# Buffers of a hybrid attention, expert and state-space kernel begin at multiples of 64 bytes

## The chip, the core and the metric

The kernel runs on one core of a Trainium2 chip. The metric is the device time of one execution in microseconds (us). A core has five engines that work side by side: TensorE (PE, matrix products; its weight loads are shown apart as PEld), VectorE (DVE), ScalarE (ACT), GpSimd (POOL) and SyncE (SP), which starts the DMA transfers. They meet through semaphores alone.

## The reference, cut to what matters

Four layers work on x, 1024 tokens of 256 features, each on a layer-normalised x and each added back to it:

```python
x = x + attention(layernorm(x), wq, wk, wv, wo)     # 16 heads of 128, 4 key heads, 4 sink keys + window of 32
x = x + experts(layernorm(x), ...)                  # 8 LoRA experts on one 704-wide gated FFN, top 2
x = x + mixer(layernorm(x), ...)                    # 512 inner, 4 heads, state 64, convolution of 4, output product
x = x + experts(layernorm(x), ...)                  # the same weights again

# attention
q = (x @ wq.T); k = (x @ wk.T); v = (x @ wv.T)
scores = q @ k.T / sqrt(128)                        # masked: k <= q and (k < 4 or k >= q - 31)
out = softmax(scores) @ v @ wo.T

# experts, for each expert e
h_e = silu(base_up + lo_up) * (base_gate + lo_gate)
mixed_h += c[:, None] * h_e;  lora_down += 2 * (c[:, None] * h_e @ down_A[e].T @ down_B[e].T)
out = mixed_h @ w_down.T + lora_down
```

All of it is in float32.

## The kernel before, in words

**Two-part products.** Most products run in TensorE's reduced float32 format (F32R). An operand is kept as a high part, rounded to that format, and a low part, the remainder. The helper `three` (line 168) issues three matmuls for a product: high with high, high with low, low with high. Line 172 is its `e.matmul`, so nearly all heavy matmuls stand under L172. Buffers of such pairs have names that end in `_hl`. ScalarE writes high parts, VectorE (in some places GpSimd) low parts. Scores, transposes and the mixer's inner products are plain float32 matmuls.

**A matmul's operands.** One operand is loaded into the array (PEld), 128 columns or so; the other is streamed, 66 to 512 columns. In the profile's names `psum<-A,B` A is streamed and B is loaded. The load for the next matmul runs beside the streaming of the present one.

**Layout.** On-chip memory is laid out by hand. Small constants, the residual x and statistics are placed by `keep` from byte 16512 of each partition on, in steps of 32. Behind them begin the large areas A_X to A_WO (lines 139 to 151), each followed by the next, and all four stages place their buffers in these areas by `at(name, shape, type, offset)`:

- A_X: `xT_hl`, the normalised and transposed x. Every stage streams it (attention also loads its first block).
- A_V: `v_hl` in attention; from the first experts' stage on `ffn_w_hl`, all weights of that stage, 61,440 bytes. The mixer's `ssd_w_out_hi` lies right behind.
- A_K: `kT`. A_KW: `k_windows`, the key blocks. A_PR: `probs`.
- A_W: `wq_hl`, and in other stages `f_ch_hl`, `f_mix_hl`, `f_sil` and mixer buffers. A_Q: `qT`, `f_um`, mixer weights and working buffers.
- A_O: `oT_hl`, before it `xg_hl`, `wk_hl`. A_P: `probs_first`, `probs_wide`. A_PT: `pT_hl`. A_WO: `wo_hl`, `wv_hl`.

**Attention** goes through 44 units, 4 key heads by 11 query blocks (the first of 128 queries, the others of 90). For a window unit GpSimd gathers a key block: 4 sink keys and three windows of 62 into `k_windows` (L773, L775); TensorE computes three score products of 66 columns (L493); VectorE masks (L697) and takes the row maximum, ScalarE exponentiates (L602), GpSimd multiplies by the reciprocal and writes three 66-wide pieces into the zeroed 126-wide rows of `probs_wide` (L788, L789); TensorE transposes them (L525), ScalarE and VectorE split the result into `pT_hl`, and TensorE multiplies with `v_hl`. Values come from `xg_hl`, a copy of x with the sink columns before each window, 10 rows of 126 columns for each part and half. Between these, the order written by hand puts the query products of the next head (xT_hl with wq_hl) and the output products (wo_hl with oT_hl).

**An experts' stage** takes 12 steps, 6 blocks of the hidden width for each of two halves of the tokens. A step issues 12 matmuls of xT_hl with ffn_w_hl (`base_x`), 12 of f_um with ffn_w_hl (`base_lora`, `second`), 6 of f_ch_hl with ffn_w_hl and 12 of ffn_w_hl with f_mix_hl (`down`). ScalarE and VectorE work on the step before meanwhile. **The mixer** has 20 input products (xT_hl with its weights), then 8 chunks of 128 tokens.

Nothing plans the order at run time: each engine runs its own written list and waits on semaphores.

## Time and profile before

| | |
|---|---|
| Median of 3 runs | 521.92 us (521.79 to 522.21) |
| The profiled execution's own time | 522.12 us |
| Its span, first to last instruction | 520.3 us |
| TensorE matmuls busy | 503.9 us, 97% of the span |
| TensorE weight loads busy | 426.7 us, 82% |
| VectorE busy | 408.8 us, 79% |
| ScalarE, GpSimd busy | 312.8 us, 145.4 us |
| Granted TensorE clock | 1.0 of full speed in all slices |

Busy time is the union of an engine's instructions; matmuls overlap, since one begins while the one before is still on its way through the array. A matmul's own duration is therefore longer than its distance to the next one; the distance (start to start) is what a sequence costs. In a view in order of time, instructions that follow each other with the same names are merged into one row with their count, and the difference of two rows' starts gives the time of the whole group between.

The reduced-precision matmuls, by the pair of names (streamed, loaded), with the count in the view of groups and the places of the two buffers modulo 64 bytes, worked out from the layout constants (offsets inside the buffers are multiples of 64, but for xg_hl, whose rows of 504 bytes begin at various places):

| Pair | Columns | Count | Places now | Places after the change |
|---|---|---|---|---|
| xT_hl, ffn_w_hl | 512 | 312 | 32, 32 | 0, 0 |
| f_um, ffn_w_hl | 512 | 288 | 0, 32 | 0, 0 |
| xT_hl, wq_hl | 512 | 192 | 32, 0 | 0, 0 |
| f_ch_hl, ffn_w_hl | 512 | 136 | 0, 32 | 0, 0 |
| xT_hl, mixer input weights (116), router (16), wk_hl (48) | 512 | 180 | 32, 0 | 0, 0 |
| wv_hl, xg_hl (60) and xT_hl (6) | 512 | 66 | 0, various or 32 | 0, 0 |
| pT_hl, v_hl | 512 | 12 | 0, 32 | 0, 0 |
| wo_hl, oT_hl | 256 | 384 | 0, 0 | 0, 0 |
| ffn_w_hl, f_mix_hl (272) and f_d_hl (48) | 256 | 320 | 32, 0 | 0, 0 |
| ssd_w_out_hi, g_hi and g_lo | 256 | 64 | 32, 0 | 0, 0 |
| pT_hl, v_hl | 360 | 120 | 0, 32 | 0, 0 |

The pairs with unequal places are 874 matmuls of 512 columns, 384 of 256 and 120 of 360.

### The profile page before, as it was taken

To read this page: it belongs to the slowest core of one execution; us is meant where nothing else is said; L and a number is where in the kernel's file an instruction comes from. 1 tells how busy PE (TensorE), PEld (TensorE's weight loads), DVE (VectorE), ACT (ScalarE), POOL (GpSimd) and SP (SyncE) were. 2 spreads that over 40 slices of the span, in tenths; PEclk is the share of its full clock that TensorE was granted. 3 is DMA by queue.
4 is the path that set the end of the run, shared out by engine and by line. 5 is a ranking of instruction groups with operands and counts; after the bars stand their busy time and mean duration, and the time that the engine had idled before them with its cause. 6 is when DMAs were issued, how large, how long until landed. Compare 5 with 4: busy or idle time off the path is not lost.

```text
span 520.3 us, 9035 instructions
## 1 busy us (share of the span) xinstructions
PE 503.9 (97%) x2950; PEld 426.7 (82%) x2951; DVE 408.8 (79%) x899; ACT 312.8 (60%) x784; POOL 145.4 (28%) x285
## 2 busy tenths in 40 slices
PE   6999999999999999999999999989999999999996
PEld 5778899999999988678888888867989768888885
DVE  5736567667666799899999899986788789899777
ACT  4656878688687754664534445899872365334342
POOL 1332424245243320020110111389554020020110
PEclk9999999999999999999999999999999999999999
DMA  7320100000000303000030000000000000000101
GB/s 273 128 82 1 42 2 2 1 1 2 2 2 15 144 2 117 31 1 1 0 141 2 2 0 1 1 2 1 1 2 1 0 0 3 1 0 1 40 2 40
DMA packets 5933, 14.17 MB, mean 27 GB/s; under 512 B 640, under 2 KB 3200, under 8 KB 5888
## 3 DMA queue, kind: packets, MB, share of 16 engines
q1 hardware_dynamic: 5888, 13.60, 7.4%
q8 instruction: 24, 0.39, 0.3%
q14 instruction: 21, 0.17, 0.1%
HBM read 12.55 MB, written 1.05 MB: 26 GB/s over the span
## 4 chain that ended last, share of the span: by engine, by line
PE 74%; DVE 15%; issue 4%; ACT 4%; DMA 1%; POOL 1%; SPq 0%; DVEq 0%; ACTq 0%; POOLq 0%
PE psum L172 57%; PE psum L493 4%; DVE xs L1993 2%; PE psum L525 2%; DVE f_t L1315 1%; PE psum L1808 1%; DMA w_raw<-in_wk 1%; PE psum L1812 1%; DVE ln_stats L214 1%; PE psum L1818 1%; PE psum L241 1%; DVE f_ch L1384 1%; DVE f_ch_hl L1398 1%; DVE xn L234 1%; DVE xT_hl L257 1%
## 5 line engine op out<-in xcount | busy, mean ns | idle before, releaser
L172 PE MATMUL psum<-xT_hl,ffn_w_hl 128*128 128x512 f32 x312 | 77.7, 395 | 0.7 <-ACT f_sil L1201 0.6
L172 PE MATMUL psum<-f_um,ffn_w_hl 128*128 128x512 f32 x288 | 72.9, 399 | 1.1 <-DVE f_t L1315 0.6
L172 PEld LDWEIGHTS psum<-xT_hl,ffn_w_hl 128*128 128x128 f32 x312 | 56.2, 188 | 13.1 <-DVE ffn_w_hl L916 1.1
L172 PEld LDWEIGHTS psum<-f_um,ffn_w_hl 128*128 128x128 f32 x288 | 53.1, 188 | 15.0 <-DVE f_um L1327 1.8
L1201 ACT ACTIVATE f_sil<-psum 128x512 f32<-128x512 f32 (+1 forms) x48 | 28.2, 596 | 48.9 <-PE psum L172 48.9
L1225 ACT ACTIVATE f_ch_hl<-f_ch 128x512 fp32r<-128x512 f32 x48 | 30.3, 632 | 42.3 <-DVE f_ch L1384 40.6
L172 PE MATMUL psum<-xT_hl,wq_hl 128*128 128x512 f32 x192 | 52.1, 407 | 0.6 <-ACT qT L593 0.6
L172 PE MATMUL psum<-wo_hl,oT_hl 128*128 128x256 f32 x384 | 50.6, 281 | 0.9 <-DVE oT_hl L726 0.6
L172 PEld LDWEIGHTS psum<-wo_hl,oT_hl 128*128 128x128 f32 x384 | 47.9, 188 | 3.4 <-DVE oT_hl L726 1.1
L593 ACT ACTIVATE qT<-psum 128x512 f32<-128x512 f32 x32 | 35.2, 1101 | 22.6 <-PE psum L172 22.6
L602 ACT ACTIVATE probs<-probs,small 120x66 f32<-120x66 f32 x120 | 39.8, 338 | 8.2 <-DVE small L703 8.2
L1315 DVE TENSOR_TENSOR f_t<-psum,f_sil 128x512 f32<-128x512 f32 (+1 forms) x48 | 33.1, 690 | 14.4 <-ACT f_sil L1201 13.3
L172 PEld LDWEIGHTS psum<-xT_hl,wq_hl 128*128 128x128 f32 x192 | 33.9, 188 | 7.7 <-issue 1.7
L788 POOL TENSOR_TENSOR probs_wide<-probs,small 120x186 f32<-120x186 f32 x40 | 19.9, 498 | 68.6 <-DVE small L683 68.6
L697 DVE TENSOR_TENSOR probs<-psum,const_bf_bits 120x198 f32<-120x198 f32 x40 | 14.5, 361 | 27.4 <-PE psum L493 27.4
L1398 DVE TENSOR_TENSOR f_ch_hl<-f_ch,f_ch_hl 128x512 fp32r<-128x512 f32 (+1 forms) x48 | 35.6, 779 | 0.1
L1384 DVE TENSOR_TENSOR f_ch<-f_t,f_wb 128x512 f32<-128x512 f32 x48 | 33.2, 691 | 1.4
L172 PEld LDWEIGHTS psum<-ffn_w_hl,f_mix_hl 128*128 128x128 f32 x240 | 30.8, 188 | 2.2 <-DVE f_mix_hl L1407 0.5
L172 PE MATMUL psum<-f_ch_hl,ffn_w_hl 128*128 128x512 f32 x120 | 32.1, 400 | 0.6 <-DVE f_ch_hl L1398 0.5
L1496 POOL MEMSET f_t<- 64x512 f32 x8 | 4.2, 519 | 101.7 <-DVE f_ch L1384 101.7
L172 PE MATMUL psum<-ffn_w_hl,f_mix_hl 128*128 128x256 f32 x240 | 31.6, 280 | 0.0
L172 PE MATMUL psum<-pT_hl,v_hl 126*128 126x360 f32 (+1 forms) x132 | 30.5, 339 | 0.0
(265 smaller groups left out, 1149.1 us busy)
## 6 DMA issues: line engine op xcount, KB each, us to landing
w_raw<-in_wq SPq DMA_DIRECT2D x4, 512.0 KB, 4.1
w_raw<-in_wo SPq DMA_DIRECT2D x4, 512.0 KB, 3.2
ffn_w_raw<-in_ffn SPq DMA_DIRECT2D x3, 576.0 KB, 5.4
ffn_w_raw_far<-in_ffn SPq DMA_DIRECT2D x3, 576.0 KB, 5.0
ssd_w_raw<-in_ssd SPq DMA_DIRECT2D x3, 512.0 KB, 5.4
x_resid<-in_x SPq DMA_DIRECT2D x2, 512.0 KB, 5.3
out_x<-x_resid SPq DMA_DIRECT2D x4, 256.0 KB, 2.1
w_raw<-in_wk SPq DMA_DIRECT2D x1, 512.0 KB, 6.3
```

What stands on the lines that cost most here:

```text
L172: i = e.matmul(dst, lhs(a), rhs(b), start=start and n == 0, stop=stop and n == len(TERMS) - 1, **kw)
L493: m = e.matmul(bank(u % 2)[0:ROWS, i * KBLK:(i + 1) * KBLK], queries_of(q, QB), kw[:, w % W_SLOTS, i, :], start=True, stop=True)
L525: m = e.transpose(bank(2 + u % 2)[0:NKEY, i * ROWS:(i + 1) * ROWS], pz[0:ROWS, u % 3, i, :], ident[0:ROWS, 0:ROWS])
L593: e.activation(qT[:, HALF * half:HALF * half + HALF, h], bank(7 if n == Q_PAIR else 6), ACT.Copy, scale=float(HD) ** -0.5).then_inc(s_qt, 1)
L602: m = e.activation(p[:, n, :], p[:, n, :], ACT.Exp, bias=NEGM[0:rows, u % 4, n:n + 1], accum_out=DEN[0:rows, u % 4, n:n + 1])
L697: e.tensor_tensor(masked, bank(u % 2)[0:rows, 0:n].rearrange("p (n k) -> p n k", n=parts), (cb[0:rows, B_M0:B_M1] if j == 0 else cb[0:rows ...
L788: e.tensor_tensor(wide, p[:, :, SINK:KBLK], spread(r, KB_WIN), ALU.mult)
L1201: e.activation(sil[at_rows, s, :], bank(i % 2)[rows, :], ACT.Silu).then_inc(FS[f"sil{s}"], 1)
L1225: e.activation(ch_hl[:, i % 2, s, HI, :], ch[:, i % 2, s, :], ACT.Copy).then_inc(FS["chh"], 1)
L1315: e.tensor_tensor(tt[rows, s, :], to_bank(i, 1)[rows, :], sil[rows, s, :], ALU.mult).then_inc(FS[f"t{s}"], 1)
L1384: e.tensor_tensor(ch[:, i % 2, s, :], tt[:, s, :], wb[:, s, half(h)], ALU.mult).then_inc(FS[f"ch{s}"], 1)
L1398: e.tensor_tensor(ch_hl[rows, i % 2, s, LO, :], ch[rows, i % 2, s, :], f32(ch_hl[rows, i % 2, s, HI, :]), ALU.subtract).then_inc(FS["chl"], 1)
```

## The change

Every large area begins at a multiple of 64 bytes; the padding before A_W shrinks by 544 bytes, so that A_W, A_Q, A_O and A_P stay at their addresses. The rows of `xg_hl` and `probs_wide` get a pitch of 128 elements (512 bytes) for their 126, those of `k_windows` a pitch of 80 elements (320 bytes) for their 66. The instructions read and write the same elements as before; only the clearing of `probs_wide` covers the padding too.

| Area | Begins at, before | after |
|---|---|---|
| A_X, A_V, A_K, A_KW | 30752, 47136, 92192, 108576 (32 modulo 64) | 32 higher (0 modulo 64) |
| A_PR | 110976 | 111488 |
| A_W, A_Q, A_O, A_P | 114432, 147200, 163584, 196352 | the same |
| A_PT, A_WO | 202944, 211136 (0 modulo 64) | 64 higher |

```diff
@@ -136,20 +136,26 @@
         minus_half = keep("minus_half", [P, NT], F32)
         small = keep("small", [P, 256], F32)
         sm = keep("softmax_small", [P, 48], F32)
-        R = base[0]
-        A_X = R
+        LINE = 64
+
+        def lines(n):
+            return -(-n // LINE) * LINE
+
+        A_X = lines(base[0])
         A_V = A_X + 2 * KB * T * 4
         A_K = A_V + 2 * NJ * KV * HD * 4
         A_KW = A_K + KV * T * 4
-        A_PR = A_KW + -(-(W_SLOTS * NB_Q * KBLK * 4) // 32) * 32
-        A_W = A_PR + -(-(3 * NB_Q * KBLK * 4) // 32) * 32 + 1056
+        KEY_PITCH, WINDOW_PITCH = lines(NKEY * 4) // 4, lines(KBLK * 4) // 4
+        A_PR = A_KW + W_SLOTS * NB_Q * WINDOW_PITCH * 4
+        A_W = A_PR + lines(3 * NB_Q * KBLK * 4) + 512
         A_Q = A_W + 32768
         A_O = A_Q + 16384
         A_P = A_O + 32768
-        A_PT = A_P + 2048 + -(-(3 * NB_Q * NKEY * 4) // 32) * 32
+        A_PT = A_P + 2048 + 3 * NB_Q * KEY_PITCH * 4
         A_WO = A_PT + 8192
         END = A_WO + 16384
         assert END <= 229344, END
+        assert all(a % LINE == 0 for a in (A_X, A_V, A_K, A_KW, A_PR, A_W, A_Q, A_O, A_P, A_PT, A_WO))
 
         ident = cf[:, C_ID:C_ID + P]
         identb = cb[:, B_ID:B_ID + P]
@@ -284,19 +290,19 @@
 
         def attention():
             kT = at("kT", [P, KV, T], F32, A_K)
-            kw = at("k_windows", [P, W_SLOTS, NB_Q, KBLK], F32, A_KW)
+            kw = at("k_windows", [P, W_SLOTS, NB_Q, WINDOW_PITCH], F32, A_KW)
             v_hl = at("v_hl", [P, 2, NJ, KV * HD], F32R, A_V)
             wq_hl = at("wq_hl", [P, 2, 2, KB, HALF], F32R, A_W)
             raw = at("w_raw", [P, 4, 1024], F32, A_W + 16384)
             qT = at("qT", [P, T, GROUP], F32, A_Q)
             oT_hl = at("oT_hl", [P, 2, GROUP, T], F32R, A_O)
-            xg_hl = at("xg_hl", [P, 2, KB, NJ - 1, NKEY], F32R, A_O)
+            xg_hl = at("xg_hl", [P, 2, KB, NJ - 1, KEY_PITCH], F32R, A_O)
             wk_hl = at("wk_hl", [P, 2, KB, KV * HD], F32R, A_O + 20480)
             wv_hl = at("wv_hl", [P, 2, KB, KV * HD], F32R, A_WO + 8192)
             wo_hl = at("wo_hl", [P, 2, 2, GROUP, D], F32R, A_WO)
             pr = at("probs", [P, 3, NB_Q, KBLK], F32, A_PR)
             pr0 = at("probs_first", [P, NB_Q0, P], F32, A_P)
-            pz = at("probs_wide", [P, 3, NB_Q, NKEY], F32, A_P + 2048)
+            pz = at("probs_wide", [P, 3, NB_Q, KEY_PITCH], F32, A_P + 2048)
             pT_hl = at("pT_hl", [P, 2, 2, 512], F32R, A_PT)
             NEGM, DEN, DENG, RDEN = (small[:, 192 + 16 * i:208 + 16 * i].rearrange("p (b h) -> p b h", b=4) for i in range(4))
 
@@ -491,7 +497,7 @@
                         for i in range(NB_Q):
                             q = Q0[j] + QB * i
                             m = e.matmul(bank(u % 2)[0:ROWS, i * KBLK:(i + 1) * KBLK], queries_of(q, QB),
-                                         kw[:, w % W_SLOTS, i, :], start=True, stop=True)
+                                         kw[:, w % W_SLOTS, i, 0:KBLK], start=True, stop=True)
                     m.then_inc(s_s, 1)
 
                 for j in range(NJ):
@@ -506,7 +512,7 @@
                         e.wait_ge(s_vlo, j - 1)
                     for k in range(KB):
                         m = three(e, bank(4 + j % 2)[0:NK[j], :],
-                                  lambda w: xT[:, w, k, 0:P] if j == 0 else xg_hl[:, w, k, j - 1, :],
+                                  lambda w: xT[:, w, k, 0:P] if j == 0 else xg_hl[:, w, k, j - 1, 0:NKEY],
                                   lambda w: wv_hl[:, w, k, :], k == 0, k == KB - 1)
                     m.then_inc(s_v, 1)
                     if j < GROUP:
@@ -523,7 +529,7 @@
                     else:
                         for i in range(NB_Q):
                             m = e.transpose(bank(2 + u % 2)[0:NKEY, i * ROWS:(i + 1) * ROWS],
-                                            pz[0:ROWS, u % 3, i, :], ident[0:ROWS, 0:ROWS])
+                                            pz[0:ROWS, u % 3, i, 0:NKEY], ident[0:ROWS, 0:ROWS])
                     m.then_inc(s_t, 1)
 
                 def p_v(u):
@@ -784,7 +790,7 @@
                     if u >= 3:
                         e.wait_ge(s_t, u - 2)
                     z = pz[0:rows, u % 3]
-                    wide = bass.AP(z.tensor, z.offset + SINK, [z.ap[0], (NKEY + QB, NB_Q), (1, KB_WIN)])
+                    wide = bass.AP(z.tensor, z.offset + SINK, [z.ap[0], (KEY_PITCH + QB, NB_Q), (1, KB_WIN)])
                     e.tensor_tensor(wide, p[:, :, SINK:KBLK], spread(r, KB_WIN), ALU.mult)
                     e.tensor_tensor(z[:, :, 0:SINK], p[:, :, 0:SINK], spread(r, SINK), ALU.mult).then_inc(s_nrm, 1)
 
```

## Rows read from the trace of the kernel before

**Rows 1.** The page: busy time, share and instructions; then slices in tenths.

```profile
PE 503.9 (97%) x2950; PEld 426.7 (82%) x2951; DVE 408.8 (79%) x899; ACT 312.8 (60%) x784; POOL 145.4 (28%) x285
...
PE   6999999999999999999999999989999999999996
...
DVE  5736567667666799899999899986788789899777
```

**Rows 2.** The page: the chain that ended last, shares by engine.

```profile
PE 74%; DVE 15%; issue 4%; ACT 4%; DMA 1%; POOL 1%; SPq 0%; DVEq 0%; ACTq 0%; POOLq 0%
```

**Rows 3.** Stretches: length, busy us (count) of PE, PEld, DVE, ACT, POOL; clock, DMA.

```profile
224.00:306.00 82.00, 81.79 (x416) 68.10 (x417) 77.43 (x135) 40.13 (x71) 9.09 (x13) 1.00 0.07 23
306.00:350.00 44.00, 42.29 (x216) 33.86 (x217) 41.49 (x78) 32.10 (x58) 15.89 (x38) 1.00 0.00 1
```

**Rows 4.** TensorE in order of time: start us, us, what; one feed-forward step.

```profile
257.32 2.89 PE L172 MATMUL psum<-xT_hl,ffn_w_hl 128*128 128x512 f32 x12
260.05 2.96 PE L172 MATMUL psum<-f_um,ffn_w_hl 128*128 128x512 f32 x12
262.86 1.56 PE L172 MATMUL psum<-f_ch_hl,ffn_w_hl 128*128 128x512 f32 x6
264.26 1.56 PE L172 MATMUL psum<-ffn_w_hl,f_mix_hl 128*128 128x256 f32 x12
265.66 0.63 PE L172 MATMUL psum<-xT_hl,ffn_w_hl 128*128 128x512 f32 x2
```

**Rows 5.** TensorE in order of time, attention.

```profile
106.86 1.53 PE L172 MATMUL psum<-wo_hl,oT_hl 128*128 128x256 f32 x12
108.22 0.66 PE L172 MATMUL psum<-pT_hl,v_hl 126*128 126x360 f32 x3
108.72 0.47 PE L525 MATMUL psum<-const_f,probs_wide 120*126 120x120 f32 x3
```

**Rows 6.** TensorE in order of time, the mixer's input products.

```profile
321.69 2.96 PE L172 MATMUL psum<-xT_hl,ssd_w_z_hl 128*128 128x512 f32 x12
324.49 0.86 PE L172 MATMUL psum<-xT_hl,ssd_w_conv_hl 128*128 128x512 f32 x3
```

**Rows 7.** Groups of instructions: busy us, mean ns, idle before.

```profile
L172 PE MATMUL psum<-xT_hl,ffn_w_hl 128*128 128x512 f32 x312 | 77.7, 395 | 0.7 <-ACT f_sil L1201 0.6
L172 PE MATMUL psum<-f_um,ffn_w_hl 128*128 128x512 f32 x288 | 72.9, 399 | 1.1 <-DVE f_t L1315 0.6 <-DVE f_um L1327 0.5
...
L1384 DVE TENSOR_TENSOR f_ch<-f_t,f_wb 128x512 f32<-128x512 f32 x48 | 33.2, 691 | 1.4
...
L788 POOL TENSOR_TENSOR probs_wide<-probs,small 120x186 f32<-120x186 f32 x40 | 19.9, 498 | 68.6 <-DVE small L683 68.6
...
L655 DVE COPY kT<-psum 128x512 f32<-128x512 f32 x8 | 5.1, 683 | 0.6 <-PE psum L172 0.6
```

**Rows 8.** TensorE in order of time, plain float32: attention, then the mixer.

```profile
36.69 1.13 PE L486 MATMUL psum<-kT,qT 128*128 128x128 f32 x8
37.58 0.70 PE L172 MATMUL psum<-wv_hl,xg_hl 128*126 128x512 f32 x2
...
364.88 1.05 PE L1808 MATMUL psum<-w_mix,x_dt 128*128 128x128 f32 x8
365.76 1.06 PE L1812 MATMUL psum<-c_exp,state 128*128 128x128 f32 x8
```

**Rows 9.** TensorE in order of time, two runs behind scores.

```profile
131.11 1.66 PE L172 MATMUL psum<-wo_hl,oT_hl 128*128 128x256 f32 x12
132.61 0.63 PE L172 MATMUL psum<-pT_hl,v_hl 128*128 128x512 f32 x2
...
134.18 1.62 PE L172 MATMUL psum<-wo_hl,oT_hl 128*128 128x256 f32 x12
135.64 0.66 PE L172 MATMUL psum<-pT_hl,v_hl 126*128 126x360 f32 x3
```

## The prediction

> **What bounds the kernel now.** I read the busy shares first, then the chain of waits, the stretches, and last single runs of matmuls on TensorE's timeline. TensorE's matmul side is busy 503.9 of 520.3 us, 97%, and nearly every slice stands at 9, while VectorE is at 79% [rows 1]. The chain of work that ended last is 74% TensorE and 15% VectorE [rows 2]. In the steady part of the first feed-forward stage TensorE is busy 81.79 of 82 us and VectorE 77.43; in the mixer's input part it is 42.29 of 44, with VectorE at 41.49 [rows 3]. So time is gained or lost here by the distance from one matmul to the next, and hardly by anything else.
>
> This distance depends on more than the columns. All four runs of one feed-forward step follow each other without a wait [rows 4]. Twelve matmuls of 512 columns, xT_hl against ffn_w_hl, take 260.05 - 257.32 = 2.73 us, 227.5 ns each. The next twelve, of the same shape, f_um against ffn_w_hl, take 2.81 us, 234.2 ns each; six of f_ch_hl take 1.40 us, 233.3 ns. Twelve of 256 columns, ffn_w_hl against f_mix_hl, take 1.40 us, 116.7 ns, where in attention twelve of wo_hl against oT_hl take 1.36 us, 113.3 ns [rows 5]. In the mixer twelve of xT_hl against ssd_w_z_hl take 2.80 us, 233.3 ns [rows 6]. (A name pair gives the streamed operand first and the loaded one second.)
>
> What sorts the fast from the slow is the two addresses modulo 64, worked out from the kernel's constants. xT_hl, ffn_w_hl, v_hl, kT and ssd_w_out_hi begin 32 bytes past a multiple of 64; wq, wk, wv, wo, oT_hl, f_um, f_ch_hl, f_mix_hl, pT_hl and the mixer's input weights begin at a multiple. Fast are xT_hl with ffn_w_hl (both at 32) and wo_hl with oT_hl (both at 0). Slow are 0 with 32 (f_um, f_ch_hl) and 32 with 0 (f_mix_hl, the mixer). Neither operand's own place explains it: ffn_w_hl is loaded in a fast and in two slow kinds, xT_hl is streamed in a fast and a slow kind. Only equal or unequal places do.
>
> **The change part by part.** It moves A_X, A_V, A_K and A_KW up by 32 bytes, and A_PT and A_WO by 64. A_PR to A_P stay put or stay at 0 modulo 64. After it every pair of the table ahead is "equal". It adds no instruction, no wait and no semaphore, and moves no DMA past a queue; the raw weights land where they did.
>
> *1. Unequal pairs of reduced-precision matmuls become equal.* By the table there are 874 of 512 columns, 384 of 256 and 120 of 360. Upper bound: each goes from the unequal to the equal pace. 512 columns: 233.8 - 227.5 = 6.3 ns (233.8 is the middle of 234.2 and 233.3), 874 x 6.3 = 5.5 us. 256 columns: 116.7 - 113.3 = 3.4 ns, 384 x 3.4 = 1.3 us. 360 columns: three take 108.72 - 108.22 = 0.50 us, 166.7 ns [rows 5], against 227.5 x 360 / 512 = 160.0, 120 x 6.7 = 0.8 us. Together 7.6 us. Lower bound: over the whole trace the equal group costs 77.7 / 312 = 249.0 ns a matmul and the unequal one 72.9 / 288 = 253.1, both with their tails [rows 7]; the difference is 4.1 ns, since equal runs too need a few matmuls to reach their pace. 874 x 4.1 = 3.6 us, half of it for 256 columns 384 x 2.0 = 0.8, seven tenths for 360 columns 120 x 2.9 = 0.3: 4.7 us. I take 5.0, 2.7 and 5.0 ns, nearer to the first steady rows but not at them, because with all neighbours equal fewer runs should have to start over: 4.4 + 1.0 + 0.6 = 6.0 us.
>
> *2. What of this reaches the end.* In the steady feed-forward stretch VectorE leaves 82 - 77.43 = 4.6 us, and the stretch holds 82 / 8.34 = 9.8 steps [rows 4] with 18 unequal matmuls of 512 columns and 12 of 256 each: 177 x 5.0 + 118 x 2.7 = 1.2 us, which passes whole. In the mixer's input part VectorE leaves 44 - 41.49 = 2.5 us, unevenly, and TensorE already waits 1.7 us; of its 116 input matmuls and the last step's 18 and 12, and f_d_hl's 24, 134 x 5.0 + 36 x 2.7 = 0.8 us, I count half. In the kernel's first 25 us (wk's 48 matmuls and wv's 6) and around the two routers (some 48), TensorE keeps waiting for inputs, means and masks: 102 x 5.0 = 0.5 us is not passed on. Off: 0.9 us. 6.0 - 0.9 = 5.1 us.
>
> *3. The gathered inputs' rows of 504 bytes become 512.* These are the 60 matmuls with xg_hl as the loaded operand and are in the 874. ScalarE writes the same number of elements into them.
>
> *4. Key blocks at 320 in place of 264 bytes, widened probabilities at 512 in place of 504.* These feed plain fp32 matmuls (240 scores, 120 transposes), for which the place shows nothing: eight unequal ones, kT against qT, take 37.58 - 36.69 = 0.89 us, 111.3 ns, and eight equal ones, w_mix against x_dt, take 365.76 - 364.88 = 0.88 us, 110.0 ns [rows 8]. I take nothing; the bound from both sides is 1.3 ns on 392 such matmuls (with the 32 of kT), 0.5 us.
>
> *5. The other engines' reads and writes at the new places.* VectorE writes 512 columns to kT at 32 in 683 ns and to f_ch at 0 in 691 [rows 7]: nothing, bounded at 8 ns on some 40 such instructions on the chain, 0.3 us either way. GpSimd's products into the widened probabilities keep their length, with 68.6 us idle before them [rows 7] to cover what differs. The one memset over them grows from 1134 to 1152 columns, under 2% of an instruction that runs while TensorE waits for its first input.
>
> The Trainium skill ("SBUF — State Buffer", section "A bandwidth-pool intuition that's wrong (but worth ruling out)") gives TensorE a second, independent read port for loading weights. By that rule the two operands' relative place would not matter and part 1 would be worth nothing. The rows on equal and unequal pairs disagree with it. Its remark in "Door 1: The DMA port swizzle (why `[64,N]` ≈ `[32,N]`)" on lines of 16 bytes speaks against the change as well, since places 0 and 32 both begin such a line; the unequal pace in the rows is not explained by it either.
>
> The profiled execution took 522.12 us, 1.8 us more than its span, and lies 0.2 us above the runs' median of 521.92. 522.12 - 5.1 = 517.0, as a median **516.8 us**.
>
> **The rivals.**
> *A. VectorE takes over.* Its share is 94% in two stretches [rows 3], and the chain already passes through it for 15% [rows 2]. A step's partial results come in the order PE, ScalarE, VectorE, PE, so a faster TensorE may only wait longer. Against it: TensorE waits 0.21 us in 82. If the feed-forward stages and the mixer give back what they gain, attention remains, 192 matmuls with wq, 60 with xg_hl and 12 + 120 of pT_hl: 264 x 5.0 + 120 x 5.0 = 1.9 us, and 0.4 us of the last stage's: 2.3 us, 519.6 us.
>
> *B. The address is not the cause.* The pace may come from the order of instructions or from what ran before. For it: one equal run, wo_hl with oT_hl at 131.11, takes 1.50 us, and one in the same position behind scores, at 134.18, 1.46 us [rows 9]: 3.6 ns apart on the eleven behind the first, with the same addresses modulo 64. So phase matters as well. Against it: all the long unequal runs shown are slow, in three stages. Time: no change, 521.9 us. This is also what the skill's rule of two independent ports would give.
>
> *C. Slower: equal runs fall into the slow phase.* The run at 131.11 shows that equal places do not guarantee the fast pace. With all buffers moved together, and the unequal runs between them gone that now reset the phase, the 312 + 384 matmuls that are fast today could stay at the slow pace: 312 x 6.7 + 384 x 3.6 = 3.5 us lost, with nothing won on the others. Half of them so gives 1.7 us, 523.6 us. It decides as soon as more matmuls leave the fast pace than enter it.
>
> *D. All of it.* Every unequal run reaches the steady equal pace and short runs start in it: 7.6 us, less 0.2 behind VectorE: 514.5 us.
>
> **How the numbers follow.** Forecast (515.2 to 518.7) 0.57; A (518.7 to 520.9) 0.16; B 0.10; C 0.09; D 0.08. A difference under 0.2% (1.04 us, about what measurements of this kernel can tell from none) counts as none. Faster: forecast, A and D, 0.81, less 0.01 of A: 0.80. None: B and the 0.01: 0.11. Slower: C, 0.09. The range takes in D and A and leaves out most of B and C: 514.2 to 520.8 us; the bounds of parts 4 and 5 (0.8 us) are within it.
>
> **What would show it.** In a feed-forward step, f_um's twelve in 2.72 to 2.76 us, f_ch_hl's six in 1.37 and f_mix_hl's twelve in 1.36 to 1.37; the mixer's twelve in 2.73; xT_hl with ffn_w_hl unchanged. Scores and transposes as before. If the feed-forward paces fall and the stretch does not, A. If they stay at 234, B, and the prediction is wrong at its root. If xT_hl's twelve rise to 2.80, C. A faster pace in plain fp32 matmuls, or other durations on VectorE, would prove parts 4 and 5 wrong.

## The result, and the profile after

The changed kernel takes 523.52 us (median of 10, 523.26 to 523.75) against 522.13 us (521.79 to 522.21) for the kernel before beside it: ratio 1.0027, interval 1.0019 to 1.0035. It is 1.4 us slower; forecast were 5.1 us gained and a range that ended at 520.8 us. The span of the profiled execution went from 520.3 to 521.6 us.

The page of the changed kernel says that the bound is the same, with a busier TensorE: 504.8 us against 503.9, VectorE 408.7 against 408.8 [rows 1], and 77% of the chain on TensorE against 74% [rows 2].

```profile
PE 504.8 (97%) x2950; PEld 428.0 (82%) x2951; DVE 408.7 (78%) x899; ACT 313.9 (60%) x784; POOL 145.6 (28%) x285
...
PE 77%; DVE 14%; issue 4%; ACT 3%; POOL 1%; DMA 1%; DVEq 0%; SPq 0%; ACTq 0%; POOLq 0%
```

Its groups (busy us, mean ns) name the loser. wo_hl with oT_hl stood at 50.6 us in the kernel before (first line below) and is at 52.1. wq, slow before, gained 0.3 us (52.1 before). The feed-forward pairs and the other engines are where they were [rows 7]. All line numbers of TensorE's helper are six higher now.

```profile
L172 PE MATMUL psum<-wo_hl,oT_hl 128*128 128x256 f32 x384 | 50.6, 281 | 0.9 <-DVE oT_hl L726 0.6
...
L178 PE MATMUL psum<-xT_hl,ffn_w_hl 128*128 128x512 f32 x312 | 78.0, 397 | 0.7 <-ACT f_sil L1207 0.6
L178 PE MATMUL psum<-f_um,ffn_w_hl 128*128 128x512 f32 x288 | 72.7, 398 | 1.1 <-DVE f_t L1321 0.6
...
L178 PE MATMUL psum<-wo_hl,oT_hl 128*128 128x256 f32 x384 | 52.1, 285 | 0.9 <-DVE oT_hl L732 0.6
L178 PE MATMUL psum<-xT_hl,wq_hl 128*128 128x512 f32 x192 | 51.8, 406 | 0.6 <-ACT qT L599 0.6
...
L794 POOL TENSOR_TENSOR probs_wide<-probs,small 120x186 f32<-120x186 f32 x40 | 20.0, 499 | 69.5 <-DVE small L689 69.5
...
L1390 DVE TENSOR_TENSOR f_ch<-f_t,f_wb 128x512 f32<-128x512 f32 x48 | 33.2, 691 | 1.4
```

TensorE in order of time (start us, us, what) shows a run's pace as the difference of two starts. In attention wo's twelve take 61.97 - 60.53 = 1.44 us, 120 ns each, where they took 1.36 [rows 5]; both runs behind scores take 1.50 and 1.51 us, where one had 1.46 [rows 9]. A feed-forward step is 266.83 - 258.45 = 8.38 us against 8.34 [rows 4]: f_um's twelve 2.80, f_ch's six 1.40, f_mix's twelve 1.41, all as slow as before, and xT_hl's twelve, said to stay, 2.77 against 2.73. In the mixer twelve take 2.75 us against 2.80 [rows 6], the only long run that gained. Eight plain records take 0.89 us against 0.88 [rows 8].

```profile
60.53 1.60 PE L178 MATMUL psum<-wo_hl,oT_hl 128*128 128x256 f32 x12
61.97 0.69 PE L178 MATMUL psum<-pT_hl,v_hl 126*128 126x360 f32 x3
...
131.44 1.67 PE L178 MATMUL psum<-wo_hl,oT_hl 128*128 128x256 f32 x12
132.94 0.86 PE L178 MATMUL psum<-pT_hl,v_hl 128*128 128x512 f32 x3
...
134.51 1.67 PE L178 MATMUL psum<-wo_hl,oT_hl 128*128 128x256 f32 x12
136.02 0.67 PE L178 MATMUL psum<-pT_hl,v_hl 126*128 126x360 f32 x3
...
258.45 2.93 PE L178 MATMUL psum<-xT_hl,ffn_w_hl 128*128 128x512 f32 x12
261.22 2.96 PE L178 MATMUL psum<-f_um,ffn_w_hl 128*128 128x512 f32 x12
264.02 1.56 PE L178 MATMUL psum<-f_ch_hl,ffn_w_hl 128*128 128x512 f32 x6
265.42 1.57 PE L178 MATMUL psum<-ffn_w_hl,f_mix_hl 128*128 128x256 f32 x12
266.83 2.93 PE L178 MATMUL psum<-xT_hl,ffn_w_hl 128*128 128x512 f32 x12
...
322.67 2.91 PE L178 MATMUL psum<-xT_hl,ssd_w_z_hl 128*128 128x512 f32 x12
325.42 0.85 PE L178 MATMUL psum<-xT_hl,ssd_w_conv_hl 128*128 128x512 f32 x3
...
365.89 1.05 PE L1814 MATMUL psum<-w_mix,x_dt 128*128 128x128 f32 x8
366.78 1.06 PE L1818 MATMUL psum<-c_exp,state 128*128 128x128 f32 x8
```

The table sorts the difference of 1.3 us by place in the program, and by pair from start-to-start distances (breaks in a run left out, the first matmuls of a run counted).

| part of the span | after - before, us | | pair | ns before, after | us |
|---|---|---|---|---|---|
| up to attention's first probabilities | -0.28 | | wo_hl, oT_hl | 115.1, 119.2 | +1.5 |
| attention | +1.20 | | xT_hl, ffn_w_hl | 229.3, 230.3 | +0.3 |
| first experts | +0.15 | | ffn_w_hl, f_mix_hl | 116.9, 117.8 | +0.2 |
| mixer | -0.02 | | xT_hl with wq, wk, mixer inputs | 233, 230 | -0.8 |
| second experts | +0.22 | | f_um and f_ch_hl, ffn_w_hl | 233.2, 233.4 | +0.1 |

Attention carries the loss and wo_hl with oT_hl carries attention's. A pair that the prediction counted among the gainers, wv_hl with xg_hl (60 matmuls), went from 231.8 to 233.0 ns.

### The profile page after: what moved, and what is told of

Its sections match the earlier page's. It is cut to its first block, busy times and chain, and to the rows that moved or that the text cites. A ratio compares the mean times of both kernels' runs of the same rounds, so it can differ in the third digit from the quotient of the medians.

```text
span 521.6 us, 9035 instructions
## 1 busy us (share of the span) xinstructions
PE 504.8 (97%) x2950; PEld 428.0 (82%) x2951; DVE 408.7 (78%) x899; ACT 313.9 (60%) x784; POOL 145.6 (28%) x285
## 4 chain that ended last, share of the span: by engine, by line
PE 77%; DVE 14%; issue 4%; ACT 3%; POOL 1%; DMA 1%; DVEq 0%; SPq 0%; ACTq 0%; POOLq 0%
PE psum L178 59%; PE psum L499 4%; PE psum L531 2%; DVE xs L1999 2%; PE psum L1814 1%; DVE f_t L1321 1%; PE psum L1818 1%; PE psum L1824 1%; DVE xT_hl L263 1%; PE psum L247 1%; DVE xn L240 1%; DVE f_ch_hl L1404 1%; PE psum L1841 1%; DVE ln_stats L220 1%; PE psum L492 1%
## 5 line engine op out<-in xcount | busy, mean ns | idle before, releaser
L178 PE MATMUL psum<-wo_hl,oT_hl 128*128 128x256 f32 x384 | 52.1, 285 | 0.9 <-DVE oT_hl L732 0.6
L178 PEld LDWEIGHTS psum<-wo_hl,oT_hl 128*128 128x128 f32 x384 | 49.3, 190 | 3.2 <-DVE oT_hl L732 1.1
```

What stands on the lines that cost most here:

```text
L178: i = e.matmul(dst, lhs(a), rhs(b), start=start and n == 0, stop=stop and n == len(TERMS) - 1, **kw)
```

## Experiments

In the expectations P is the theory that the distance between the two operands' places decides the pace. Its rival, S in the first texts and H in a later one, is that what runs ahead decides. D is VectorE as the next bound. "Distance" is from here on the loaded operand's address less the streamed one's, modulo 256. "Fast" and "slow" say of a run of wo's twelve whether its fourth to eleventh start-to-start times have a mean of 113 to 114 ns or of 117 to 118; the first three are left out, since many runs take them slower.

**wo_hl alone moved, in the kernel before.**

```diff
-        A_WO = A_PT + 8192
+        A_WO = A_PT + 8192 + 64
```

> The kernel before with A_WO alone 64 bytes higher; nothing else of the change. Theory P: the runs of wo_hl with oT_hl go from 1.36 to 1.43 us, all others keep their pace, +1.6 us, 523.7 us. Rival S (the loss comes from equal neighbours around these runs): the runs stay at 1.36 us, 522.1 us. Rival W (the widened rows cost the time): 522.1 us.

Measured 523.41 us, ratio 1.0027 (1.0016 to 1.0037): the whole loss of the change from one address. Only the pair wo_hl, oT_hl moved, from 115.1 to 119.4 ns (+1.5 us), all others stayed within 0.2 us. In this kernel's TensorE rows the run takes 62.09 - 60.66 = 1.43 us.

```profile
60.66 1.59 PE L172 MATMUL psum<-wo_hl,oT_hl 128*128 128x256 f32 x12
62.09 0.67 PE L172 MATMUL psum<-pT_hl,v_hl 126*128 126x360 f32 x3
```

Both operands are multiples of 64 in both kernels, so "equal modulo 64" says nothing here, and the prediction's rule is wrong.

**wo_hl put back, in the changed kernel.**

```diff
-        A_WO = A_PT + 8192
+        A_WO = A_PT + 8192 + 448
```

> The changed kernel with A_WO 448 bytes higher, so that wo_hl lies 192 bytes past a multiple of 512 again, as before the change (oT_hl lies 256 past one). Theory P (the place of the streamed operand relative to the loaded one counts over a period longer than 64 bytes, some hundred bytes, so that the move of wo_hl by 64 bytes against oT_hl lost the fast pace): a long run of wo_hl with oT_hl goes from 1.43 to 1.36 us for its twelve, the 384 matmuls give back 1.5 us, 522.0 us. Rival S (the slow phase is a matter of how runs follow each other, not of wo_hl's place): the runs stay at 1.43 us, 523.5 us.

Measured 522.69 us, ratio 1.0013 (1.0004 to 1.0022), between the two. Half of the loss came back. wo's mean is 116.9 ns: 17 of its 19 unbroken runs of twelve stand at 117 to 118 ns, where the kernel before has 18 at 113 to 114. The run in the rows takes 69.27 - 67.86 = 1.41 us. The distance is the same as before, so there is a second cause.

```profile
67.86 1.58 PE L178 MATMUL psum<-wo_hl,oT_hl 128*128 128x256 f32 x12
69.27 0.67 PE L178 MATMUL psum<-pT_hl,v_hl 126*128 126x360 f32 x3
```

**The pitches alone, in the kernel before** (the three new row lengths, each area kept at its old place modulo 512).

```diff
-            kw = at("k_windows", [P, W_SLOTS, NB_Q, KBLK], F32, A_KW)
+            kw = at("k_windows", [P, W_SLOTS, NB_Q, WINDOW_PITCH], F32, A_KW)
...
-            xg_hl = at("xg_hl", [P, 2, KB, NJ - 1, NKEY], F32R, A_O)
+            xg_hl = at("xg_hl", [P, 2, KB, NJ - 1, KEY_PITCH], F32R, A_O)
...
-            pz = at("probs_wide", [P, 3, NB_Q, NKEY], F32, A_P + 2048)
+            pz = at("probs_wide", [P, 3, NB_Q, KEY_PITCH], F32, A_P + 2048)
```

> The kernel before with the three wider row pitches alone (512 bytes for the gathered inputs and the widened probabilities, 320 for the key blocks); the areas keep their places modulo 512. Theory P: only the 60 matmuls with xg_hl may move, within 0.1 us: 522.1 us. Rival W (the pitches cost what the change lost, through scores, transposes or GpSimd): 523.5 us.

Measured 522.10 us against 521.98, ratio 1.0002 (0.9993 to 1.0011). No cost of the pitches can be told from none, and wo stays fast in 18 of 19 runs.

**A map of distances.** A micro kernel, traced once at a granted clock of 0.998: runs of 24 reduced-precision matmuls, each with its own weight load.

```diff
+                for k in range(n):
+                    m = e.matmul(PS[:, g % 6, 0:cols], pool[:, st:st + P], pool[:, mv:mv + cols], start=k == 0, stop=k == n - 1)
```

> Computes nothing of the reference; copies x to the output, and beside it issues groups of 24 reduced-precision matmuls, first of 512 and then of 256 streamed columns, every one with its own weight load of 128 columns. Between groups stands one matmul of 64 columns. The streamed operand lies at one place, the loaded one 64 KB and 0, 32, 64, ... 992 bytes further; then both are moved together by 32, 64, 128, 256 bytes. Theory P: the steady distance takes a few values, 226.7, 230 and 233.3 ns for 512 columns, 113.3, 116.7 and 120 ns for 256, and they depend on the relative place with a period above 64 bytes; moving both together changes nothing. Theory E of the prediction (equal or unequal modulo 64): two values that alternate from step to step. Rival N (no dependence on addresses): one value throughout.

The rows of this kernel: one matmul of 64 columns as a mark, then the 24. At distance 0 (first two rows) the 24 of 512 columns take 54.65 - 49.09 = 5.56 us, at 32 they take 5.68. With 256 columns distance 0 costs 278.62 - 275.67 = 2.95 us and distance 64 costs 2.82: the best place for 512 columns is among the worst two for 256.

```profile
49.09 5.71 PE L148 MATMUL psum<-operands 128*128 128x512 f32 x24
54.65 0.19 PE L146 MATMUL psum<-operands 128*128 128x64 f32 x1
54.67 5.84 PE L148 MATMUL psum<-operands 128*128 128x512 f32 x24
60.35 0.19 PE L146 MATMUL psum<-operands 128*128 128x64 f32 x1
...
275.67 3.12 PE L148 MATMUL psum<-operands 128*128 128x256 f32 x24
278.62 0.20 PE L146 MATMUL psum<-operands 128*128 128x64 f32 x1
...
281.61 2.98 PE L148 MATMUL psum<-operands 128*128 128x256 f32 x24
284.43 0.19 PE L146 MATMUL psum<-operands 128*128 128x64 f32 x1
```

Mean start-to-start time of the last 16, in ns, with the 360 columns of the next kernel:

| distance | 0 | 32 | 64 | 96 | 128 | 160 | 192 | 224 |
|---|---|---|---|---|---|---|---|---|
| 512 columns | 226.7 | 233.3 | 233.3 | 234.3 | 232.9 | 233.2 | 228.7 | 233.3 |
| 360 columns | 164.4 | 166.6 | 166.7 | 165.3 | 166.7 | 163.3 | 166.7 | 164.4 |
| 256 columns | 120.0 | 118.3 | 113.3 | 117.2 | 118.7 | 120.2 | 117.8 | 116.6 |

It repeats every 256 bytes up to 992 (tried for 512 and 256 columns). Moving both operands together, tried at distances 0 and 192, changes it by 0.8 ns at most. In steps finer than 32 bytes the next kernel has 226.7 ns at distance 240 for 512 columns, and 232.4 at 4. Most pairs of the two kernels stand near it:

| pair | distance before, after | ns by the map | ns measured |
|---|---|---|---|
| xT_hl, ffn_w_hl | 0, 0 | 226.7, 226.7 | 229.3, 230.3 |
| f_um and f_ch_hl, ffn_w_hl | 32, 64 | 233.3, 233.3 | 233.2, 233.4 |
| xT_hl with wq, wk, mixer inputs | 224, 192 | 233.3, 228.7 | 233, 230 |
| ffn_w_hl, f_mix_hl | 224, 192 | 116.6, 117.8 | 116.9, 117.8 |
| wo_hl, oT_hl | 64, 0 | 113.3, 120.0 | 115.1, 119.2 |

One pair does not: wv_hl with xg_hl stands at distance 0 after the change, where the map has 226.7 ns, and takes 233.0 in its runs of six.

**The feed-forward step, and plain matmuls, by distance.** Micro kernel, traced once, with the step of [rows 4]: u is the distance of f_um and f_ch_hl, f that of f_mix_hl.

```diff
+                for q, (mv, st, cols, n, plain) in enumerate(parts):
+                    as_ = (lambda a: a.bitcast(F32)) if plain else (lambda a: a)
```

> Computes nothing of the reference; copies x to the output and issues groups of matmuls: single kinds of 24 (360 columns, 512 columns at finer distances, 128 columns plain and reduced) at distances 0 to 224; then three feed-forward steps in a row (12 x 512 at distance 0, 12 x 512 and 6 x 512 at a distance u, 12 x 256 at a distance f) for u of 0, 32, 64, 192 and f of 0 to 224; then four attention steps in a row (6 x 512 at distance a, 12 x 256 at b, 3 x 360 at 0, 9 plain) for a of 0, 192, 224 and b of 0 to 224. Theory P: the feed-forward step is shortest for u = 0 and f = 64, 8.0 to 8.1 us, against 8.35 for u = 32, f = 224 (before) and 8.4 for u = 64, f = 192 (the change); plain matmuls show one pace. Rival S: the step's time does not follow the sum of the steady paces, and differs more between orders than between distances.

Three steps between two marks, in its rows, take 255.75 - 230.93 = 24.82 us at u 0, f 64; 581.62 - 556.53 = 25.09 at the old places (32, 224); 757.96 - 732.77 = 25.19 at the new ones (64, 192).

```profile
230.93 24.98 PE L149 MATMUL psum<-operands 128*128 128x512 f32 x126
255.75 0.20 PE L144 MATMUL psum<-operands 128*128 128x64 f32 x1
...
556.53 25.26 PE L149 MATMUL psum<-operands 128*128 128x512 f32 x126
581.62 0.19 PE L144 MATMUL psum<-operands 128*128 128x64 f32 x1
...
732.77 25.35 PE L149 MATMUL psum<-operands 128*128 128x512 f32 x126
757.96 0.19 PE L144 MATMUL psum<-operands 128*128 128x64 f32 x1
```

The middle step alone takes 8.33 us at the old places and 8.38 at the new, which is what the two whole kernels show (8.34, 8.38). The expected 8.0 to 8.1 us at u 0, f 64 was missed: the middle step takes 8.24 there and is shortest, 8.22, at u 0 with f 96 or 192. Theory P does not hold for the last run of the step. Behind six matmuls at u 0 the twelve of 256 columns at f 64 take 1.41 us, behind six at u 64 they take 1.37, where the map's 113.3 ns would make 1.36. The gain of the 512 columns is there: f_um's twelve take 2.72 us at u 0 and 2.80 at 32 or 64.

Records of 128 columns follow each other in 111.6 to 111.7 ns at every distance, plain or reduced. Four steps in attention's order take 21.06 to 21.37 us; wo's distance 64 is 0.15 to 0.21 us shorter than 0, and 192 is as short as 64 or shorter behind two of the three places of the run ahead.

**Places chosen by the map, in the changed kernel.** xT_hl, v_hl, wq_hl, ffn_w_hl, f_um, f_ch_hl, oT_hl and the mixer's input weights all at 0 modulo 256, wo_hl and ssd_w_out at 192, f_mix_hl at 64 (core of the edit; the tiles behind f_mix_hl move with it).

```diff
-        A_X = lines(base[0])
+        A_X = -(-base[0] // 256) * 256
...
-        A_WO = A_PT + 8192
+        A_WO = A_PT + 8192 + 192
...
-            mix_hl = at(f"{tag}_mix_hl", [P, 2, 2, HALF], F32R, A_W + 16384)
+            mix_hl = at(f"{tag}_mix_hl", [P, 2, 2, HALF], F32R, A_W + 16448)
```

> The changed kernel with places chosen by the map of the run before (distance of the loaded operand from the streamed one modulo 256): A_X, A_V, A_W, A_Q, A_O, A_PT at multiples of 256, so that all pairs of 512 columns lie at distance 0; f_mix_hl and its neighbours and the mixer's buffers behind them 64 bytes higher, wo_hl 64 bytes below a multiple, wv_hl at one, ssd_w_out_hi and _lo 64 below one, so that the pairs of 256 columns lie at distance 64. Theory P (the distance modulo 256 sets the pace): f_um's twelve in 2.73 us, f_mix_hl's in 1.36, the mixer's in 2.73; 7 us less by the steady paces, 5 us after what runs need to settle: 517 us, bounds 514.5 and 520. Rival S (how runs follow each other decides, and short runs never settle): the paces stay between, 521 us or more.

Measured 521.06 us against 522.10, ratio 0.9980 (0.9971 to 0.9989): faster than both kernels, but far from the 517 us of theory P and outside its bounds of 514.5 to 520; rival S had said 521 or more. f_um went from 233.3 to 228.1 ns (-1.4 us), f_ch_hl to 228.2 (-0.6), wq to 230.7 (-0.35), the mixer's inputs and wk to 228.5 (-0.6 together). A step in the second experts' stage takes 464.74 - 456.50 = 8.24 us, f_um's twelve 2.72, f_ch's six 1.36: the figures that the prediction expected of the change.

The pairs of 256 columns gained nothing. f_mix's twelve in this step take 1.41 us, not 1.36. Of the pair's 20 runs of twelve five reach 113 ns, the one at 455.13 among them (1.37 us); over the kernel the pair stands at 117.0 ns, where it had 116.9 before and the map has 113.3 for its distance of 64. The step in the micro kernel has the same times at the same places (1.41 of 8.24 us). wo stands at 115.9 ns against 115.1: 13 of its 19 runs take five matmuls at 116 to 123 ns before they reach 113, and three never do. f_d_hl, left at distance 0, went from 117.1 to 119.2. TensorE's busy time fell from 503.94 to 501.66 us, and the span by 1.2.

```profile
455.13 1.53 PE L178 MATMUL psum<-ffn_w_hl,f_mix_hl 128*128 128x256 f32 x12
456.50 2.91 PE L178 MATMUL psum<-xT_hl,ffn_w_hl 128*128 128x512 f32 x12
459.25 2.88 PE L178 MATMUL psum<-f_um,ffn_w_hl 128*128 128x512 f32 x12
461.97 1.52 PE L178 MATMUL psum<-f_ch_hl,ffn_w_hl 128*128 128x512 f32 x6
463.33 1.58 PE L178 MATMUL psum<-ffn_w_hl,f_mix_hl 128*128 128x256 f32 x12
464.74 2.91 PE L178 MATMUL psum<-xT_hl,ffn_w_hl 128*128 128x512 f32 x12
```

The second stage became 0.70 us shorter, the first, with the same matmuls, 0.12. The stretch of the first stage (length, busy us and count by engine; the kernel before, then this one) shows where it went: TensorE was busy 85.36 of 85.57 us and is busy 84.74 of 85.45. Of 0.62 us that it saves, 0.50 is idle time now, beside a VectorE at 80.70 in both.

```profile
231.66:317.23 85.57, 85.36 (x446) 71.02 (x445) 80.70 (x141) 39.67 (x69) 8.49 (x11) 1.00 0.06 22
...
231.22:316.67 85.45, 84.74 (x447) 71.11 (x445) 80.70 (x141) 39.66 (x70) 8.51 (x11) 1.00 0.06 22
```

**Is that VectorE?** The last kernel with four of the first stage's low parts made on GpSimd.

```diff
-                    if 1 <= i <= 4:
-                        split(i + 3)
...
+                if first:
+                    e.wait_ge(s_fwl, 4)
+                    for n in range(4, NPIECE):
+                        w_lo(e, n)
```

> The kernel with chosen places, and the low parts of the last four weight pieces (4.5 us of VectorE in the first experts' stage) made by GpSimd. Theory D (the first experts' stage hardly gained from the chosen places because VectorE holds it back there): that stage falls from 85.45 to 84.7 us and the kernel by 0.7 us, 520.3 us. Rival (the stage is held by something else, or GpSimd's reads slow VectorE): no change, 521.1 us, or slower.

Measured 523.19 us, ratio 1.0023 (1.0014 to 1.0033): 2.1 us slower than without the edit. The rows of GpSimd, VectorE and TensorE at that place (idle time and what ended it in brackets) show a product on VectorE (f_t times f_wb), 0.69 us elsewhere, lasting 2.68 us: it starts 0.56 us after GpSimd's operation of 2.69 us and ends 0.55 us behind it. TensorE waits 1.70 us for what follows from it.

```profile
226.74 2.69 POOL L922 TENSOR_TENSOR ffn_w_hl<-ffn_w_raw_far,ffn_w_hl 128x1152 fp32r<-128x1152 f32 x1 [2.09 <-ACT ffn_w_hl L918]
...
227.30 2.68 DVE L1390 TENSOR_TENSOR f_ch<-f_t,f_wb 128x512 f32<-128x512 f32 x1
...
232.12 1.63 PE L178 MATMUL psum<-f_ch_hl,ffn_w_hl 128*128 128x512 f32 x6 [1.70 <-DVE f_ch_hl L1404]
```

The edit gave VectorE less to do and held it up elsewhere, so it doesn't settle how much VectorE alone takes of the first stage's gain; that stays open.

**What holds wo's runs at 118 ns: the distance of wq_hl?** In the kernel before, wq_hl at distance 192 (the changed kernel's), then at 0.

```diff
-            wq_hl = at("wq_hl", [P, 2, 2, KB, HALF], F32R, A_W)
+            wq_hl = at("wq_hl", [P, 2, 2, KB, HALF], F32R, A_W - 32)
```

> The kernel before with wq_hl alone 32 bytes lower, so that the loaded operand of the query products lies 192 past the streamed one modulo 256, as after the change, and wo_hl stays at its old distance of 64 from oT_hl. Theory H (the place decides, but a run of twelve can also stay in the state in which the run before it leaves it): the query products fall from 233 to 230 ns, and the runs of wo_hl with oT_hl behind them rise from 113.3 to 117.7 ns although their own addresses did not change; +0.4 us in attention, 522.4 us. Rival P (distance alone): the runs of wo_hl stay at 113.3 ns and the kernel gains 0.3 us, 521.7 us.

Measured 522.17 us against 521.94 (0.9996 to 1.0014). The time can't be told from none, the runs can: wq gained 0.2 us by its own distance, and wo, none of whose addresses moved, lost 0.36, since 11 of its 19 runs of twelve now stand at 117 to 118 ns. Its run at 72.17 takes 1.42 us; the same run of the kernel before (first two rows) takes 1.38.

```profile
72.31 1.55 PE L172 MATMUL psum<-wo_hl,oT_hl 128*128 128x256 f32 x12
73.69 0.66 PE L172 MATMUL psum<-pT_hl,v_hl 126*128 126x360 f32 x3
...
72.17 1.58 PE L172 MATMUL psum<-wo_hl,oT_hl 128*128 128x256 f32 x12
73.59 0.65 PE L172 MATMUL psum<-pT_hl,v_hl 126*128 126x360 f32 x3
```

```diff
+            wq_hl = at("wq_hl", [P, 2, 2, KB, HALF], F32R, A_W - 224)
```

> The kernel before with wq_hl alone 224 bytes lower: distance 0 for the query products. Theory H: the query products settle towards 226.7 ns, 0.4 us less, and the runs of wo_hl behind them come out partly at 113.3 and partly at 117.7; between 521.6 and 522.1 us. Rival P: 0.4 to 0.8 us less, 521.3 us, with all of wo_hl's runs at 113.3.

Measured 521.78 us against 521.94, ratio 0.9996 (0.9987 to 1.0005): wq 230.5 ns, -0.4 us, wo fast in 18 of 19. The mean is in the direction of the map and too small for the timing to tell.

**wo_hl at distance 192 in the chosen places.**

```diff
-        A_WO = A_PT + 8192 + 192
+        A_WO = A_PT + 8192 + 64
```

> The kernel with chosen places, but wo_hl 64 bytes above a multiple of 256 instead of 64 below (distance 192 from oT_hl in place of 64). By the steady paces of the map it loses 4.4 ns on each of 384 matmuls, 1.7 us, 522.7 us (P). By the measured attention steps of the last map both distances take 3.89 to 3.91 us a step: no change, 521.1 us (H).

Measured 521.52 us, ratio 0.9991 (0.9982 to 1.0), between the two forecasts and 0.5 us above the kernel with chosen places. wo stands at 117.7 ns, which is the map's 117.8, and all 19 runs do; the loss is smaller than P's 1.7 us because wo had stood at 115.9 and not at 113.3.

**Both put back in the changed kernel**, and **pT_hl alone moved in the kernel before.**

```diff
-        A_WO = A_PT + 8192
+        A_WO = A_PT + 8192 + 448
...
-            wq_hl = at("wq_hl", [P, 2, 2, KB, HALF], F32R, A_W)
+            wq_hl = at("wq_hl", [P, 2, 2, KB, HALF], F32R, A_W - 192)
```

> The changed kernel with wo_hl back at 64 modulo 256 from oT_hl (as in e1_wo_back) and wq_hl down by 192 bytes, so that xT_hl and wq_hl are at distance 0 modulo 256 in place of 192. Of wo's 19 unbroken runs of twelve, 18 are at 113 to 114 ns in the kernel before, 2 in e1_wo_back (the others at 117 to 118). Theory HQ: what the runs of wq leave behind at distance 192 holds wo's runs in the slower state, as e6_wq_down_32 showed for 11 of 19. Then most of the 19 are fast again, wo gains 384 x 1.8 = 0.7 us on e1_wo_back, and the median is 522.0 us. Theory HV: it is the neighbour pT_hl with v_hl, at distance 64 in place of 96. Then 15 or more stay slow and the median is 522.5 to 522.7 us. Theory I: both neighbours count: in between, 6 to 14 slow, 522.2 to 522.4 us.

Measured 522.81 us, ratio 1.0013 (1.0004 to 1.0022), with 18 of 19 slow. HQ falls: with wq_hl at distance 0 wo's runs are slow here and fast in the kernel before.

```diff
-        A_PT = A_P + 2048 + -(-(3 * NB_Q * NKEY * 4) // 32) * 32
-        A_WO = A_PT + 8192
+        A_PT = A_P + 2048 + -(-(3 * NB_Q * NKEY * 4) // 32) * 32 + 32
+        A_WO = A_PT + 8192 + 224
```

> The kernel before with pT_hl up by 32 bytes and all else at its place modulo 256: v_hl stands at distance 64 from pT_hl in place of 96, wo_hl stays at 64 from oT_hl, wq_hl at 224 from xT_hl. By the map 120 matmuls of 360 columns go from 165.3 to 166.7 ns, 0.2 us slower. Theory HQ: the neighbour pT_hl has no hold on wo's runs: 18 of 19 fast as before, median 522.1 us. Theory HV: wo's runs fall into the slower state behind pT_hl's: 10 or more of 19 at 117 to 118 ns, 0.4 to 0.8 us slower, 522.5 to 522.9 us. Theory I: a few of them, 522.2 to 522.4 us.

Measured 522.08 us, ratio 1.0 (0.9991 to 1.0009), 18 of 19 fast. HV falls too. One thing among others that e7 and e10 (wq_hl at distance 0, in the kernel before and in the changed one) do not share is xT_hl's own place against the place of oT_hl: 32 there, 64 here.

**The run ahead, by both of its places.** Micro kernel, traced once: six of 512 columns (streamed at a, loaded at a + e), then wo's twelve at distance 64, then plain ones. An entry of its list (cut after the first repetition of a 0, e 224) gives the streamed place, the loaded one, columns, count and whether they are plain.

```diff
+    GROUPS = [[(1024, 1248, 512, 6, 0), (4288, 8192, 256, 12, 0), (0, 0, 128, 9, 1), ...
```

> A micro kernel that computes nothing of the reference (it copies x to the output) and times matmuls alone. 32 groups of six repetitions; each repetition is six reduced-precision matmuls of 512 columns with the streamed operand at a and the loaded one at a + e modulo 256, then at once twelve of 256 columns with the streamed operand at 192 and the loaded one at 0 (wo's places in the kernel before, distance 64), then nine plain ones of 128. a goes through 0, 32 .. 224, e through 224, 192, 0 and 64. Attention in the kernels had, for wq's run ahead of wo's: before a 32, e 224 (wo fast in 17 or 18 of 18), e7 32, 0 (fast in 17 of 18), e5b 0, 0 (15), e6 32, 192 (7), e1 64, 192 (1), e10 64, 0 (0). Theory N, the neighbour: the places of the run ahead decide in which state the twelve start, and they stay in it: here the twelve take 113 to 114 ns each behind a 32 with e 224 or 0 and a 0 with e 0, and 117 to 118 behind a 64 with either e. Theory O, something else in the changed kernels (another engine's accesses, or the operands beyond the place modulo 256): the twelve take the same behind every a and e, 113.3 ns as the long runs at distance 64 did.

The twelve in the last five repetitions, mean of the fourth to eleventh start-to-start time in ns:

| a | 0 | 32 | 64 | 96 | 128 | 160 | 192 | 224 |
|---|---|---|---|---|---|---|---|---|
| e 224 | 117.7 | 113.2 | 117.8 | 113.2 | 113.4 | 113.3 | 113.3 | 117.7 |
| e 192 | 113.8 | 113.3 | 117.7 | 113.8 | 113.3 | 115.2 | 113.3 | 115.1 |
| e 0 | 113.7 | 113.3 | 117.7 | 113.4 | 113.3 | 117.8 | 117.8 | 115.2 |
| e 64 | 113.3 | 117.8 | 116.0 | 113.3 | 113.4 | 113.2 | 113.3 | 117.7 |

The groups of 256 columns in the stretches of a 32 and of a 64, both at e 224, differ by 4 ns in the mean duration of one (busy us, mean ns), with nothing changed in the twelve themselves:

```profile
L149 PE MATMUL psum<-operands 128*128 128x256 f32 x72 | 9.1, 276 | 0.0
...
L149 PE MATMUL psum<-operands 128*128 128x256 f32 x72 | 9.4, 280 | 0.0
```

Theory N holds in five of the six cases that the kernels tried: behind a 32 with e 224 (before) or 0, and a 0 with e 0, fast; behind a 64 with e 192 or 0, slow, as 17 and 18 of 19 runs in the changed kernel with wo_hl put back. The sixth, a 32 with e 192, is fast in the micro kernel, and in the kernel 11 of 19 runs behind it were slow. So the run ahead has a hold on the pace, and both of its places count. Theory O, one pace behind every run, is out.

The single times show how. Behind a 64 with e 224 all twelve stay at 116 to 120 ns. Behind a 192 with e 224 the first three take 118, 124 and 119 before the rest take 112 to 115, and behind a 160 with e 192 the first five take 118 to 124. A run thus settles at 113 after up to five slower matmuls or stays near 118 to its end. Why these places and not others stays open.

## Why the prediction was wrong

*The bound was read rightly for a slower TensorE.* 1.3 us more of matmul spacing made the span 1.3 us longer. A faster one passes only in part, see part 2.

*Part 1 failed, at "only equal or unequal places do".* The rule was fitted to two values, 0 and 32 modulo 64, and the pairs shown happened to stand at distances 0, 32, 64 and 224 modulo 256. Distance 0 (xT_hl, ffn_w_hl) is fast for 512 columns and 64 (wo_hl, oT_hl) for 256; modulo 64 both look "equal". Making everything equal modulo 64 took f_um and f_ch_hl from 32 to 64, which is no faster: 424 of the 874 matmuls. Most of the others of 512 columns went from 224 to 192 and gained 0.8 us, 2 to 4 ns each where the map has 4.6; that their short runs are the reason is not shown. The 60 with xg_hl, which were to gain 5.0 ns, lost 1.2. So the term of 4.4 us was 0.7. The term of 1.0 us for 256 columns was a loss of 0.2, f_mix_hl's distance 192 being the slower one, and the term of 0.6 us for 360 columns came out as nothing (166.2 and 166.9 ns; the map has 163 to 167 at all distances). The prediction's equal pace of 160.0 ns had been scaled from 512 columns, and no run shows it. A term was put at nothing without a reason: the pair with wo_hl was the fast one for 256 columns in the rows, and the sum put no price on moving its address by 64. It cost 1.5 us, shown by moving it alone.

The second, independent read port for weights that the Trainium skill gives TensorE ("SBUF — State Buffer", section "A bandwidth-pool intuition that's wrong (but worth ruling out)") was rightly not followed: the map shows 226.7 to 234.3 ns for the same instruction, by nothing but the two operands' distance. The period of the effect was wrong, not that there is one.

*Part 2* (0.9 us of 6.0 not reaching the end) could not be seen in the changed kernel. With the chosen places it was right in kind and its share too small: of 2.3 us less busy time 1.2 us reached the end. "Passes whole" failed in the first feed-forward stage, where 0.62 us of busy time gave 0.12 us, while the second became 0.70 shorter. That looks like rival A in one stage; that VectorE is what holds it is not shown.

*Parts 4 and 5* were right, and of part 3 that the row pitch costs nothing: pitches 0.1 us within an interval that holds zero; plain records 111.6 ns everywhere; VectorE's and GpSimd's durations unchanged (691 and 499 ns against 691 and 498).

*The rivals.* B, no effect of the address and 521.9 us, falls with the runs in which one address moves and the time with it; but its observation that equal addresses have two paces was the second cause. C gave the right sign and nearly the time (523.6 against 523.52). Its mechanism, that matmuls of equal places lose their pace when their neighbours change, exists: it is the 0.7 us that stay when wo_hl is put back, and e6 and m3 show it alone. The larger part has another cause, distance 0; in the changed kernel the two are not added, since at that distance all 19 runs are at 120 ns anyway. Its sign of being right, xT_hl's twelve in 2.80 us, did not come (2.77), so that its time fits is luck. C had 0.09 only because "all the long unequal runs are slow" was taken for proof of the rule. D, which took the rule further, falls with it.

## What to carry to other kernels

A rule read off an existing layout holds only for the distances that the layout happens to contain: before moving buffers by it, tabulate every pair at the widest modulus that the addresses allow, and price the pairs at the good pace that will move as well as the others. Where TensorE is the bound and each 4-byte matmul loads its own weights, choose the distance between the streamed and the loaded operand by width from a measured map, one pair at a time. Here 0 modulo 256 for 512 columns brought 5 ns a matmul in the kernel too. For 256 columns the map's 64 held in one pair of the kernel before and brought nothing when a second pair was moved to it, so time such a pair behind the run that really stands ahead of it. Expect a few nanoseconds a matmul (here 0.2% of the kernel), and look for the part that another engine or the run ahead takes back.

## What the hardware showed that I had not expected

- In long runs the pace of a reduced-precision matmul with its own weight load depends on the distance of its two operands with a period of 256 bytes: 226.7 to 234.3 ns for 512 columns, 113.3 to 120.2 for 256, and not at all for 128 (111.6 to 111.7).
- At distance 64 a run of twelve of 256 columns settles at 113.3 ns within its first five matmuls or stays at 117.8 to its end. In the micro kernel the places of the run ahead choose which; in the kernels they did in five of six cases.
- A VectorE product of two on-chip operands, 0.69 us, took 2.68 us beside a GpSimd operation of 2.69 us that had begun 0.56 us earlier; a small cast, 0.18 us elsewhere, took 2.13 beside another. The Trainium skill ("SBUF — State Buffer", section "🔬 SBUF: two separate sides") describes such a lock for a VectorE operation with two on-chip inputs against a GpSimd operation that reads on-chip memory, and the product in this trace agrees.
